# Moving the next token block's normalization and transposes later, and splitting the running sum of h*C into two tiles, in an adaLN + Mamba + mixture-of-experts kernel

## The chip, the cores and the metric

The kernel runs on one core of one Trainium2 chip. The metric is the device time of one execution in microseconds. TensorE (PE), VectorE (DVE), ScalarE (ACT), GpSimd (POOL) and SyncE (SP, which only issues DMAs) each run their own instruction stream in order and wait for one another through semaphores.

## The reference, cut to what matters

x has 4 sequences of 2048 tokens with 512 channels, in float32. Each sequence has six modulation vectors. The computation is

```
h  = layernorm(x) * (1 + ca) + sa
x1 = x + ga * mamba(h)
out = x1 + gb * moe(layernorm(x1) * (1 + cb) + sb)
```

In `mamba`, `z = h @ W_in` is split into val and gate, val goes through a convolution over 3 tokens and a SiLU and becomes u, and `B`, `C`, `Delta` are projections of u. For each of 512 channels and 16 states n:

```
abar_t = exp(Delta*A);   bbar_t = expm1(Delta*A)/(Delta*A + 1e-6) * Delta * B_t
h_t = abar_t * h_{t-1} + bbar_t * u_t
y_t = sum over n of h_t * C_t
out = (y * silu(gate)) @ W_out + residual
```

`moe` has one shared and eight routed experts (hidden size 256, exact GELU), two routed experts per token, every expert computed for all tokens and weighted by its gate.

## The kernel before, in words

Tokens are worked on in 16 blocks of 512 (index q, or H in the code). Channels lie on the 128 partitions, in 4 groups. The scan works on tiles of 128 x 1024: one unit is 1024 (channel group, token) columns, it has 16 states, and there are 32 units. So there are 512 tiles, numbered c. The program is a list of slots, one for each c, and each engine's stream holds for each slot its part of the scan and its part of everything else. A window is 32 slots (two units, one block's worth of other work). I call slot r of window H the one with c = 32H + r. The other work in window H is for several blocks at once (`steps_of`): projections of block qa = H+2, preparation of block qn = H+3, and output projection and experts of blocks qf = H-2 and qp = H-3. In windows 2 to 13 one slot of the scan carries one step of the other work; before window 2 and after window 13 the ratio differs (`PACE`). In the first windows POOL also scales weights ("fold", L1418). The first two and the last two token blocks form scan blocks of their own with two half tiles per instruction.

What one tile c goes through:

- ACT (`act_batch`), four tiles at a time. A batch first makes four squares (L754), then two logarithms over two tiles each (L761), then for each tile `exps` (L763): an exponential (L767), a tanh into `th` (L772, three buffers) and `abar` (L776). Each switch between kinds of function costs a table load. Batch w of a window (w = 0 to 7) runs about the time of slots 4w to 4w+3 and makes the tiles that are four slots further on. Named places within a batch ("start", "half squared", "squared", "half logs", "logs", 0, 1, 2, 3) are where `act_steps` puts the other work. Before its tanh of tile c, ACT waits for `thinv_done`: POOL has used the buffer's tile before.
- POOL (`pool_slot`) in slot c: multiplies the finished state of tile c-1 by its C row (`times_C`, L1352/L1355; in those scan blocks that hand their state on, a small copy L1348 stands before it), then Newton and `pool_steps` work such as `gating` (L1441: hidden activations times gate rows, in slots 18, 19, 22, 23, 24, 29, 30, 31), then `weight(c+2)` (L1379: `inv` times `th`). In slots 1 and 17 `gate_y` follows (L1372: the sum times silu(gate)). Last comes `add_to_y(c-1)`: a DMA that POOL issues and that adds the tile h*C to the tile `ysum` (L1366; the first state of a unit is copied, L1363). Each add waits for the one before it to have landed.
- PE (`pe_slot`) in slot c broadcasts row c+1 of B into PSUM (L1150) when the scan of c-1 is done; then `pe_jobs` gives the matmuls of that slot. They share four PSUM banks. `bank_of` and `before` are worked out when the program is built, from `bank_held_to`, an estimate of when each job's result has been taken; a job waits until the result before it in its bank has been taken.
- DVE (`dve_slot`) in slot c: times weight (L1179), times ratio (L1186), B row of c+1 times u (L1167), the scan of c (L1197), plus abar for c+1 (L1173), then other steps.
- SP issues each load at its place in the list, behind waits. In slot 24 it loads a C row once the tile before is multiplied (L680), then a gate row (`load_gate_row`, L564, waits for the fifth `gating`, that of slot 24), and then `load_w1(qf, 8)` (L544), the last expert's first matrix, which the two PE jobs ("w1", 16) and ("w1", 17) of slot 26 need.

The part that moves is the preparation of block qn: ACT normalizes its x in `xa` (L964, at batch 5 "start"), PE transposes it in slots 21 and 22 (jobs "t", L1051), and ACT takes the four transposes to `hT` (L825, `take_t`, batch 5 "logs" and place 1). The job ("w1", qf, 12) of slot 23 gets the PSUM bank of transpose 2, ("w1", qf, 13) that of transpose 3. The transposed block is needed by the "val" jobs of slot 31.

Of the kernel before, what the change touches and what calls it, by code (L numbers as in the profile page):

```python
# [8 lines left out]
ALU = mybir.AluOpType  # L9
# [15 lines left out]
def adaln_mamba_moe(nc, x, W_val, W_gate, taps, W_BC, W_deltaT, delta_base, W_tau, A_log, W_out, gate_W, W1, b1, W2, b2,  # L25
# [52 lines left out]
    with ExitStack() as ctx:  # L78
# [41 lines left out]
        th = sb("th", [P, 3, TB])  # L120
        abar = sb("abar", [P, 4, TB])
        hs = sb("hs", [P, 4, TB])
        ysum = sb("ysum", [P, TB])
# [263 lines left out]
        y_summed, y_gated, carry_done = sem("y_summed"), sem("y_gated"), sem("carry_done")  # L387
# [355 lines left out]
        def act_batch(act, batch):  # L743
# [19 lines left out]
            def exps(c):  # L763
                u = unit(c)
                act.wait_ge(ln_done, c + 1)
                for cols, g in parts(u):
                    ins = s.activation(inv[:, c % 6, cols], inv[:, c % 6, cols], ACT.Exp, scale=-1.0,  # L767
                                       bias=ln_coef[:, c % N, g:g + 1])
                ins.then_inc(inv_done, 1)
                ge(act, thinv_done, c - 2)  # L770
                for cols, g in parts(u):
                    ins = s.activation(th[:, c % 3, cols], delta[:, u % 2, cols], ACT.Tanh, scale=halfA[:, c % N, g:g + 1])  # L772
# [43 lines left out]
        def act_steps(act, H, w, place):  # L816
            s = nc.scalar
            qa, qn, qf, qp = H + 2, H + 3, H - 2, H - 3

# [122 lines left out]
            if w == 6:  # L942
                if place == "start":
                    take_w1(qf, 6)
                if place == "half squared":
                    take_w1(qf, 7)
                if place == 0:
                    take_w1(qf, 8)
            if w == 5:
                if place == "logs":  # L950
                    take_t(qn, (0, 1))
                    gelu(qf, 1)
                if place == 1:
                    take_t(qn, (2, 3))
                if place == "start" and has(qn):
                    act.wait_ge(a_rstd, qn + 1)
                    for tt in range(TPB):
                        ins = s.activation(rstdA[:, tt, 1:2], momA[:, tt, 0:1], ACT.Identity, scale=rstdA[:, tt, 0:1])
                    ins.then_inc(a_shift, 1)
                    act.wait_ge(a_shift, 2 * qn + 1)  # L960
                    s.activation(rstdA[:, :, 1], rstdA[:, :, 1], ACT.Identity, scale=-1.0).then_inc(a_shift, 1)
                    act.wait_ge(a_shift, 2 * qn + 2)
                    for tt in range(TPB):
                        ins = s.activation(xa[:, tt, :], xa[:, tt, :], ACT.Identity, bias=rstdA[:, tt, 1:2], scale=rstdA[:, tt, 0:1])  # L964
                    ins.then_inc(a_xn, 1)
            if w == 7:
                if place == "start":
                    gelu(qf, 2)

        def pe_jobs(H, r):
# [18 lines left out]
        def bank_held_to(j, at):  # L991
# [5 lines left out]
            held = {"t": (22.2, 22.3, 23.1, 23.2), "val": (1.5, 2.5, 3.5, 3.9), "gate": (8.3, 8.4, 9.5, 9.6), "p": (10.9, 11, 11.4, 11.5),  # L997
# [37 lines left out]
        def pe_steps(pe, H, r):  # L1035
# [6 lines left out]
            def job(j):  # L1042
# [5 lines left out]
                if kind == "t":  # L1048
                    pe.wait_ge(a_xn, q + 1)
# [106 lines left out]
        def dve_slot(dve, c):  # L1156
# [180 lines left out]
        def pool_slot(pool, c):  # L1337
# [20 lines left out]
            def add_to_y(c):  # L1358
                if 0 <= c < NC:
                    pool.wait_ge(hC_done, c + 1)  # L1360
                    if c % N == 0:
                        ge(pool, y_gated, unit(c))
                        gp_.dma_start(ysum[:], hs[:, c % 4, :]).then_inc(y_summed, 16)  # L1363
                    else:
                        pool.wait_ge(y_summed, 16 * c)
                        gp_.dma_start(ysum[:], hs[:, c % 4, :], accum_op=ALU.add).then_inc(y_summed, 16)  # L1366

            def gate_y(u):
                if 0 <= u < NU:
                    pool.wait_ge(y_summed, 16 * N * (u + 1))  # L1370
                    pool.wait_ge(gate_ld, 16 * (u + 1))
                    gp_.tensor_tensor(gy[:], ysum[:], gy[:], ALU.mult).then_inc(y_gated, 1)  # L1372

            def weight(c):
                if 0 <= c < NC:
# [3 lines left out]
                    gp_.tensor_tensor(inv[:, c % 6, :], inv[:, c % 6, :], th[:, c % 3, :], ALU.mult).then_inc(thinv_done, 1)  # L1379
# [14 lines left out]
            times_C(c - 1)  # L1394

# [9 lines left out]
            add_to_y(c - 1)  # L1405
# [148 lines left out]
```

## Time and profile before

| | us |
|---|---|
| median of 3 runs | 4772.27 (4767.54 to 4777.16) |
| the profiled execution, own time | 4775.98 |
| its span, first to last instruction | 4774.2 |
| mean granted TensorE clock | 0.885 |

Busy time of each engine over the span: DVE 4043.6 us (85%), ACT 3976.1 (83%), PE 3867.6 (81%), POOL 3651.3 (76%). A window in the middle takes 262 to 269 us. The table and the busy shares are averages over stages with different limits: setup (to 220 us), windows 0 and 1 with the weight scaling (to 770 us), windows 2 to 12 (to 3680 us), window 13 (to 3937 us), the faster-paced end (to 4560 us) and the last expert work (to 4774 us). In the rows further down, a bracket after an instruction is the time that its engine sat idle before it, and what ended that.

### The profile page before, as it was taken

Reading aid. Unit: us, or ns where it says so; the run is one execution under the profiler, and the core shown is the slowest. Engines: PE = TensorE matmul, PEld = TensorE weight load, DVE = VectorE, ACT = ScalarE, POOL = GpSimd, SP = SyncE. Lnnn points to the kernel's source line nnn. Section 1 sums busy time; section 2 is a strip of 40 time slices with the busy share of each in tenths; the row PEclk is TensorE's granted clock in tenths of the full one; section 3 lists DMA queues with packets and bytes.
Section 4 is the critical chain, followed back from the end, with each engine's and each line's share of the span. In section 5 each row is a group of like instructions: output and inputs, shape, how many; then the busy total and the mean of one; then the engine's idle time right before and its main releaser. Section 6 shows DMA issues by size and latency. Waiting matters only on the chain.

```text
span 4774.2 us, 37136 instructions
## 1 busy us (share of the span) xinstructions
PE 3867.6 (81%) x9708; PEld 1620.4 (34%) x9708; DVE 4043.6 (85%) x3896; ACT 3976.1 (83%) x4394; POOL 3651.3 (76%) x2304
## 2 busy tenths in 40 slices
PE   6624514989898888899898988899898977989889
PEld 3201101334333333333343333333333333333344
DVE  1388799999998989999999989999998998788820
ACT  2688798999989898989989898999899897978811
POOL 0499988888888888788888888788888887767621
PEclk7856756999999999999999999899999998989889
DMA  3678868878787878788787878888887886667541
GB/s 131 218 232 260 247 151 223 223 230 254 223 254 217 257 224 258 213 246 249 224 258 218 250 220 259 238 254 228 238 255 218 240 227 160 181 169 193 154 132 66
DMA packets 352221, 1037.19 MB, mean 217 GB/s; under 512 B 41253, under 2 KB 44389, under 8 KB 344710
## 3 DMA queue, kind: packets, MB, share of 16 engines
q1 hardware_dynamic: 278282, 766.35, 47.0%
q0 software_dynamic: 73728, 268.47, 28.4%
q8 instruction: 78, 1.28, 0.1%
q14 instruction: 133, 1.09, 0.1%
HBM read 639.74 MB, written 126.51 MB: 160 GB/s over the span
## 4 chain that ended last, share of the span: by engine, by line
PE 27%; ACT 21%; issue 14%; DVE 12%; POOL 10%; DMA 8%; SPq 0%; POOLq 0%; DVEq 0%; ACTq 0%
PE ps L1113 11%; PE ps L1132 8%; DMA ysum<-hs 6%; ACT inv L761 4%; PE ps L1083 4%; POOL inv L1379 3%; DVE ps L1179 3%; DVE ps L1167 2%; ACT th L772 2%; DVE ps L1173 2%; ACT inv L754 2%; ACT abar L776 2%; ACT inv L767 2%; POOL hs L1352 2%; DVE hs L1197 1%
## 5 line engine op out<-in xcount | busy, mean ns | idle before, releaser
L1379 POOL TENSOR_TENSOR inv<-inv,th 128x1024 f32<-128x1024 f32 x512 | 1261.4, 2464 | 203.7 <-ACT th L772 202.6
L1113 PE MATMUL ps<-hf,w1r 128*128 128x512 f32 x2304 | 1133.5, 646 | 135.0 <-ACT hT L825 69.9
L1352 POOL TENSOR_TENSOR hs<-hs,Cb 128x1024 f32<-128x1024 f32 x384 | 972.2, 2532 | 34.0 <-DVE hs L1197 17.5
L1150 PE MATMUL ps<-Brow,pick 48*128 48x512 bf16 x1024 | 342.5, 418 | 621.9 <-DVE hs L1197 620.9
L1132 PE MATMUL ps<-w2r,hid 128*128 128x512 f32 x1776 | 815.1, 606 | 0.9 <-DVE x L1236 0.9
L1167 DVE SCALAR_TENSOR_TENSOR ps<-ps,us 128x1024 f32<-128x1024 f32 x512 | 628.4, 1227 | 215.7 <-PE ps L1150 215.4
L754 ACT ACTIVATE inv<-nrd,kappa 128x1024 f32<-128x1024 f32 (+1 forms) x640 | 578.5, 967 | 188.2 <-DVE ps L1179 187.9
L1366 POOL DMA_DIRECT2D ysum<-hs x480 | 437.2, 911 | 355.4 <-DMA ysum<-hs 344.4
L1113 PEld LDWEIGHTS ps<-hf,w1r 128*128 128x128 f32 x2304 | 459.3, 206 | 730.3 <-issue 596.8
L1186 DVE SCALAR_TENSOR_TENSOR ps<-nrd,inv_kappa,ps 128x1024 f32<-128x1024 f32 (+1 forms) x640 | 675.2, 1073 | 15.6
L1197 DVE TENSOR_TENSOR_SCAN hs<-abar,carry,ps 128x512 f32<-128x512 f32 (+1 forms) x384 | 683.6, 1802 | 0.3
L776 ACT ACTIVATE abar<-delta,negA 128x1024 f32<-128x1024 f32 (+1 forms) x640 | 606.5, 967 | 83.2 <-DVE hs L1197 83.2
L1179 DVE SCALAR_TENSOR_TENSOR ps<-ps,inv 128x1024 f32<-128x1024 f32 x512 | 628.0, 1226 | 46.2 <-POOL inv L1379 23.1
L1173 DVE SCALAR_TENSOR_TENSOR ps<-abar,ps 128x1024 f32<-128x1024 f32 x512 | 618.8, 1209 | 21.2 <-ACT abar L776 21.1
L767 ACT ACTIVATE inv<-inv,ln_coef 128x1024 f32<-128x1024 f32 (+1 forms) x640 | 607.9, 969 | 1.5
L772 ACT ACTIVATE th<-delta,halfA 128x1024 f32<-128x1024 f32 (+1 forms) x640 | 605.9, 966 | 0.2 <-POOL inv L1379 0.2
L1197 DVE TENSOR_TENSOR_SCAN hs<-abar,ps 128x1024 f32<-128x1024 f32 (+1 forms) x256 | 511.7, 2009 | 0.3
L1132 PEld LDWEIGHTS ps<-w2r,hid 128*128 128x128 f32 x1776 | 333.1, 192 | 452.7 <-issue 447.5
L761 ACT ACTIVATE inv<-inv 128x2048 f32<-128x2048 f32 x256 | 479.2, 1903 | 1.4
L1150 PEld LDWEIGHTS ps<-Brow,pick 48*128 48x128 bf16 x1024 | 58.5, 96 | 982.0 <-DVE hs L1197 765.0
L1355 POOL TENSOR_TENSOR hs<-hs,Cb 128x1024 f32<-128x1024 f32 x128 | 310.8, 2428 | 36.2 <-DVE hs L1197 28.1
L1236 DVE TENSOR_TENSOR x<-ps,x 128x512 f32<-128x512 f32 x256 | 172.0, 683 | 171.6 <-PE ps L1132 150.8
(155 smaller groups left out, 5052.9 us busy)
## 6 DMA issues: line engine op xcount, KB each, us to landing
ysum<-hs POOLq DMA_DIRECT2D x512, 512.0 KB, 5.5
Cb<-c_rows SPq DMA_DIRECT2D x384, 512.0 KB, 4.5
w1r<-in_W SPq DMA_DIRECT2D x144, 512.0 KB, 5.7
w2r<-w_scaled SPq DMA_DIRECT2D x141, 512.0 KB, 7.3
Cb<-c_rows SPq DMA_DIRECT2D x128, 256.0 KB, 3.9
gbc<-expert_gates SPq DMA_DIRECT2D x128, 256.0 KB, 5.2
aw<-in_W_val SPq DMA_DIRECT2D x64, 256.0 KB, 6.5
xa<-in_x SPq DMA_DIRECT2D x32, 512.0 KB, 7.4
```

The lines of the kernel that those rows point to most:

```text
L767: ins = s.activation(inv[:, c % 6, cols], inv[:, c % 6, cols], ACT.Exp, scale=-1.0, bias=ln_coef[:, c % N, g:g + 1])
L772: ins = s.activation(th[:, c % 3, cols], delta[:, u % 2, cols], ACT.Tanh, scale=halfA[:, c % N, g:g + 1])
L776: ins = s.activation(abar[:, c % 4, cols], delta[:, u % 2, cols], ACT.Exp, scale=negA[:, c % N, g:g + 1])
L1113: mm = t.matmul(o, w1r[:, n % 2, k, h * P:(h + 1) * P], hf[:, k, :], start=(k == 0), stop=(k == G - 1))
L1132: mm = t.matmul(o, hidden(e)[:, h, tt * P:(tt + 1) * P], (last_w2(e) if q == NQ - 1 and grp == 1 else w2r[:, e % 3])[:, h, :], start=(grp ...
L1167: v.scalar_tensor_tensor(X(c), X(c), 1.0, us[:, u % 2, :], ALU.mult, ALU.mult).then_inc(uB_done, 1)
L1173: v.scalar_tensor_tensor(X(c), abar[:, c % 4, :], 1.0, X(c), ALU.add, ALU.mult).then_inc(p1_done, 1)
L1179: v.scalar_tensor_tensor(X(c), X(c), 1.0, inv[:, c % 6, :], ALU.mult, ALU.mult).then_inc(pw_done, 1)
L1186: ins = v.scalar_tensor_tensor(X(c)[:, cols], nrd[:, u % 2, cols], inv_kappa[:, c % N, g:g + 1], X(c)[:, cols], ALU.add, ALU.mult)
L1197: ins = v.tensor_tensor_scan(hs[:, c % 4, cols], abar[:, c % 4, cols], X(c)[:, cols], 0.0 if begins(u) else carry[:, g, c % N:c % N + 1], ...
L1352: gp_.tensor_tensor(hs[:, c % 4, :], hs[:, c % 4, :], Cb[:, c % 2, :], ALU.mult).then_inc(hC_done, 1)
L1379: gp_.tensor_tensor(inv[:, c % 6, :], inv[:, c % 6, :], th[:, c % 3, :], ALU.mult).then_inc(thinv_done, 1)
```

## The change

- ACT: the xa normalization is split. Its small statistics steps go from batch 5 "start" to batch 5 place 1; the four tile normalizations go two to batch 5 place 3 and two to batch 6 place 2; the four `take_t` go to batch 7, "squared" and "logs".
- PE: the transposes go from slots 21 and 22 to slots 28 and 29, with new estimates for their banks. As a result ("w1", 12) gets the bank of ("w2", 0) from slot 20, and transposes 2 and 3 in slot 29 get the banks of transposes 0 and 1 from slot 28.
- `th` has two buffers instead of three, so that ACT's tanh of tile c waits for POOL's weight of tile c-2 instead of c-3.
- `ysum` has two tiles, for even and odd states, each with a semaphore. An add waits for the add two states before. `gate_y` first adds the two tiles on POOL (one more 128 x 1024 operation for each unit) and then multiplies.
- POOL: `add_to_y(c-1)` moves from the end of the slot to directly behind `times_C(c-1)`, except in slots 1 and 17.

```diff
-        th = sb("th", [P, 3, TB])
+        th = sb("th", [P, 2, TB])
-        ysum = sb("ysum", [P, TB])
+        ysum = sb("ysum", [P, 2, TB])
...
-                ge(act, thinv_done, c - 2)
+                ge(act, thinv_done, c - 1)
...
+            def normalize_x(q, tts):
+                if has(q):
+                    act.wait_ge(a_shift, 2 * q + 2)
+                    for tt in tts:
+                        ins = s.activation(xa[:, tt, :], xa[:, tt, :], ACT.Identity, bias=rstdA[:, tt, 1:2], scale=rstdA[:, tt, 0:1])
+                    ins.then_inc(a_xn, 1)
...
+                if place == 2:
+                    normalize_x(qn, (2, 3))
             if w == 5:
                 if place == "logs":
-                    take_t(qn, (0, 1))
                     gelu(qf, 1)
-                if place == 1:
-                    take_t(qn, (2, 3))
-                if place == "start" and has(qn):
+                if place == 3:
+                    normalize_x(qn, (0, 1))
+                if place == 1 and has(qn):
...
             if w == 7:
+                if place == "squared":
+                    take_t(qn, (0, 1))
+                if place == "logs":
+                    take_t(qn, (2, 3))
...
-                20: [("w1", qf, 11), ("w2", qf, 0)], 21: [("w2", qf, 1), ("t", qn, 0), ("t", qn, 1)],
-                22: [("w2", qf, 2), ("t", qn, 2), ("t", qn, 3)], 23: [("w2", qf, 3), ("w1", qf, 12)],
+                20: [("w1", qf, 11), ("w2", qf, 0)], 21: [("w2", qf, 1)],
+                22: [("w2", qf, 2)], 23: [("w2", qf, 3), ("w1", qf, 12)],
-                27: [("w2", qf, 4)], 28: [("w2", qf, 5)], 29: [("w2", qf, 6)],
+                27: [("w2", qf, 4)], 28: [("w2", qf, 5), ("t", qn, 0), ("t", qn, 1)], 29: [("w2", qf, 6), ("t", qn, 2), ("t", qn, 3)],
...
-            held = {"t": (22.2, 22.3, 23.1, 23.2),
+            held = {"t": (29.2, 29.3, 30.1, 30.2),
...
-                        dve.wait_ge(y_summed, 16 * (c - 3))
+                        dve.wait_ge(y_summed[c % 2], 16 * (c // 2 - 1))
...
             def gate_y(u):
                 if 0 <= u < NU:
-                    pool.wait_ge(y_summed, 16 * N * (u + 1))
+                    for odd in range(2):
+                        pool.wait_ge(y_summed[odd], 16 * (N // 2) * (u + 1))
+                    gp_.tensor_tensor(ysum[:, 0, :], ysum[:, 0, :], ysum[:, 1, :], ALU.add).then_inc(y_joined, 1)
+                    pool.wait_ge(y_joined, u + 1)
                     pool.wait_ge(gate_ld, 16 * (u + 1))
...
             times_C(c - 1)
+            if r not in (1, 17):
+                add_to_y(c - 1)
...
             if r in (1, 17):
                 gate_y(c // N - 1)
-            add_to_y(c - 1)
+                add_to_y(c - 1)
```

## Rows read from the trace of the kernel before

**Rows 1.** Busy time of windows 2 to 12 (start:end us, length, PE, PEld, DVE, ACT, POOL; clock, DMA)

```profile
770.00:3680.00 2910.00, 2577.92 (x6506) 1069.99 (x6504) 2737.74 (x2463) 2636.46 (x2637) 2425.84 (x1509) 0.93 0.83 238
```

**Rows 2.** What DVE waited for, windows 2 to 12: us, times, longest

```profile
DVE ps L1167 <- PE ps L1150: 105.6, 41, 7.8
DVE ps L1173 <- ACT abar L776: 21.1, 11, 4.1
DVE ps L1179 <- POOL inv L1379: 15.6, 15, 2.0
```

**Rows 3.** Timeline of DVE, slot 23 of windows 2, 8 and 12

```profile
973.95 1.23 DVE L1167 SCALAR_TENSOR_TENSOR ps<-ps,us 128x1024 f32<-128x1024 f32 x1 [6.25 <-PE ps L1150]
...
2549.68 1.23 DVE L1173 SCALAR_TENSOR_TENSOR ps<-abar,ps 128x1024 f32<-128x1024 f32 x1 [2.04 <-ACT abar L776]
2560.68 1.23 DVE L1167 SCALAR_TENSOR_TENSOR ps<-ps,us 128x1024 f32<-128x1024 f32 x1 [6.71 <-PE ps L1150]
...
3617.71 1.23 DVE L1167 SCALAR_TENSOR_TENSOR ps<-ps,us 128x1024 f32<-128x1024 f32 x1 [7.80 <-PE ps L1150]
```

**Rows 4.** Timeline of PE and ACT around slot 23 of window 8

```profile
2526.37 2.93 ACT L964 ACTIVATE xa<-xa,rstdA 128x512 f32<-128x512 f32 x4
2539.42 1.43 ACT L825 ACTIVATE hT<-ps,modc 128x512 f32<-128x512 f32 x2
2553.62 1.43 ACT L825 ACTIVATE hT<-ps,modc 128x512 f32<-128x512 f32 x2
2554.43 5.67 PE L1113 MATMUL ps<-hf,w1r 128*128 128x512 f32 x8 [6.99 <-ACT hT L825]
```

**Rows 5.** Timeline of all engines, slots 20 to 27 of window 13

```profile
3841.84 2.28 DVE L1197 TENSOR_TENSOR_SCAN hs<-abar,ps 128x1024 f32<-128x1024 f32 x1
3849.12 1.23 DVE L1167 SCALAR_TENSOR_TENSOR ps<-ps,us 128x1024 f32<-128x1024 f32 x1 [1.23 <-PE ps L1150]
3892.96 1.23 DVE L1179 SCALAR_TENSOR_TENSOR ps<-ps,inv 128x1024 f32<-128x1024 f32 x1 [2.20 <-POOL inv L1379]
3898.89 1.23 DVE L1167 SCALAR_TENSOR_TENSOR ps<-ps,us 128x1024 f32<-128x1024 f32 x1 [3.37 <-PE ps L1150]
3842.68 1.15 ACT L772 ACTIVATE th<-delta,halfA 128x1024 f32<-128x1024 f32 x1
3864.33 2.37 POOL L1379 TENSOR_TENSOR inv<-inv,th 128x1024 f32<-128x1024 f32 x1 [1.40 <-ACT th L772]
3878.21 2.36 POOL L1441 TENSOR_TENSOR hid<-hid,gbc 128x1024 f32<-128x1024 f32 x1
3880.97 0.45 SPq L544 DMA_DIRECT2D w1r<-in_W  x1
3889.41 8.91 PE L1113 MATMUL ps<-hf,w1r 128*128 128x512 f32 x16 [6.22 <-DMA w1r<-in_W]
```

**Rows 6.** What POOL waited for, whole span: us, times, longest

```profile
POOL ysum L1366 <- DMA ysum<-hs: 344.4, 134, 7.2
POOL ysum L1363 <- POOL gy L1372: 20.0, 31, 1.0
```

**Rows 7.** Groups of POOL instructions (busy us, mean ns | idle before)

```profile
L1372 POOL TENSOR_TENSOR gy<-ysum,gy 128x1024 f32<-128x1024 f32 x32 | 77.3, 2416 | 11.2 <-DMA ysum<-hs 11.1
```

**Rows 8.** Timeline, window 8: POOL slots 15 and 19, ACT and DVE slot 20

```profile
2491.46 0.90 POOL L1366 DMA_DIRECT2D ysum<-hs  x1 [1.79 <-DMA ysum<-hs]
2520.41 2.35 POOL L1379 TENSOR_TENSOR inv<-inv,th 128x1024 f32<-128x1024 f32 x1
2522.03 1.14 ACT L772 ACTIVATE th<-delta,halfA 128x1024 f32<-128x1024 f32 x1
2523.27 2.28 DVE L1197 TENSOR_TENSOR_SCAN hs<-abar,ps 128x1024 f32<-128x1024 f32 x1
```

**Rows 9.** What POOL waited for, 220 to 514 us: us, times, longest

```profile
POOL ysum L1366 <- DMA ysum<-hs: 10.8, 8, 2.2
```

**Rows 10.** The chain of waits: start us, us, what (window 11)

```profile
3357.39 10.21 DMA w1r<-in_W
```

More of the change, by code:

```diff
@@ L386, in adaln_mamba_moe @@
             sem("B_ready"), sem("uB_done"), sem("abar_plus_1_done"), sem("weighted_done"), sem("bu_done"), sem("scan_done"))
-        y_summed, y_gated, carry_done = sem("y_summed"), sem("y_gated"), sem("carry_done")
+        y_summed = [sem("even_states_summed"), sem("odd_states_summed")]
+        y_joined, y_gated, carry_done = sem("y_joined"), sem("y_gated"), sem("carry_done")
         a_stat, a_log, a_rstd, a_shift, a_xn = (
@@ L769, in exps @@
                 ins.then_inc(inv_done, 1)
-                ge(act, thinv_done, c - 2)
+                ge(act, thinv_done, c - 1)
                 for cols, g in parts(u):
-                    ins = s.activation(th[:, c % 3, cols], delta[:, u % 2, cols], ACT.Tanh, scale=halfA[:, c % N, g:g + 1])
+                    ins = s.activation(th[:, c % 2, cols], delta[:, u % 2, cols], ACT.Tanh, scale=halfA[:, c % N, g:g + 1])
                 ins.then_inc(th_done, 1)
@@ L961, in act_steps @@
                     s.activation(rstdA[:, :, 1], rstdA[:, :, 1], ACT.Identity, scale=-1.0).then_inc(a_shift, 1)
[L962 to L965, printed above, removed]
             if w == 7:
@@ L996, in bank_held_to @@
                 return at + 1.95
-            held = {"t": (22.2, 22.3, 23.1, 23.2), "val": (1.5, 2.5, 3.5, 3.9), "gate": (8.3, 8.4, 9.5, 9.6), "p": (10.9, 11, 11.4, 11.5),
+            held = {"t": (29.2, 29.3, 30.1, 30.2), "val": (1.5, 2.5, 3.5, 3.9), "gate": (8.3, 8.4, 9.5, 9.6), "p": (10.9, 11, 11.4, 11.5),
                     "bc": (14.6,), "t2": (12, 12.1, 12.6, 12.7), "log": (14.95,), "gT": (15.9,),
@@ L1048, in job @@
                 if kind == "t":
-                    pe.wait_ge(a_xn, q + 1)
+                    pe.wait_ge(a_xn, 2 * (q + 1))
                     for tt in range(TPB):
@@ L1360, in add_to_y @@
                     pool.wait_ge(hC_done, c + 1)
-                    if c % N == 0:
+                    if c % N < 2:
                         ge(pool, y_gated, unit(c))
-                        gp_.dma_start(ysum[:], hs[:, c % 4, :]).then_inc(y_summed, 16)
+                        gp_.dma_start(ysum[:, c % 2, :], hs[:, c % 4, :]).then_inc(y_summed[c % 2], 16)
                     else:
-                        pool.wait_ge(y_summed, 16 * c)
-                        gp_.dma_start(ysum[:], hs[:, c % 4, :], accum_op=ALU.add).then_inc(y_summed, 16)
+                        pool.wait_ge(y_summed[c % 2], 16 * (c // 2))
+                        gp_.dma_start(ysum[:, c % 2, :], hs[:, c % 4, :], accum_op=ALU.add).then_inc(y_summed[c % 2], 16)
             def gate_y(u):
                 if 0 <= u < NU:
-                    pool.wait_ge(y_summed, 16 * N * (u + 1))
+                    for odd in range(2):
+                        pool.wait_ge(y_summed[odd], 16 * (N // 2) * (u + 1))
+                    gp_.tensor_tensor(ysum[:, 0, :], ysum[:, 0, :], ysum[:, 1, :], ALU.add).then_inc(y_joined, 1)
+                    pool.wait_ge(y_joined, u + 1)
                     pool.wait_ge(gate_ld, 16 * (u + 1))
-                    gp_.tensor_tensor(gy[:], ysum[:], gy[:], ALU.mult).then_inc(y_gated, 1)
+                    gp_.tensor_tensor(gy[:], ysum[:, 0, :], gy[:], ALU.mult).then_inc(y_gated, 1)
             def weight(c):
@@ L1378, in weight @@
                     pool.wait_ge(th_done, c + 1)
-                    gp_.tensor_tensor(inv[:, c % 6, :], inv[:, c % 6, :], th[:, c % 3, :], ALU.mult).then_inc(thinv_done, 1)
+                    gp_.tensor_tensor(inv[:, c % 6, :], inv[:, c % 6, :], th[:, c % 2, :], ALU.mult).then_inc(thinv_done, 1)
             def newton(u, place):
```

## The prediction

> **What bounds the kernel now.** I read the busy times of windows 2 to 12 first: they take 2910 us of the 4774, and DVE is busy 2738 of them [rows 1]. The four elementwise operations and the scan of a slot are fixed work on DVE, so only DVE's idle time there can be won. The view of what DVE waited for says how much: 105.6 us for PE's B row, 21.1 us for ACT's abar, 15.6 us for POOL's weight, 142.3 us in all [rows 2]. POOL's waits for the sum's DMA look larger, 344.4 us over the span [rows 6], but they are idle time of an engine that is seldom waited for, and count only where they come through in those 15.6 us.
>
> Then the timeline of DVE, to see where in a window the waits lie. In each of the eleven windows slot 23 holds one pair: a wait for abar and a wait for the B row; in window 8 they are 2.04 and 6.71 us, and the B row wait is 6.25 us in window 2 and 7.80 in window 12 [rows 3]. The abar waits sum to the 21.1 us; the eleven B row waits of slot 23 sum to 72.5 of the 105.6 us. Together 93.6 us, 8.5 a window. The other 33.1 us are small waits: 6.5 us in slot 26, 5.4 in slot 20, the rest in slots 5, 6, 13, 15 and 19.
>
> The cause is in the timelines of PE and ACT. PE idles 6.99 us until ACT has taken transposes 2 and 3, because job ("w1", 12) needs that bank, and the B row is queued behind that job. ACT is late since its batch 5 starts with 2.93 us of normalization and has 1.33 us of `take_t` before its first tanh (two instructions that share 1.43 us with overlap) [rows 4].
>
> **What the change does, part by part.**
>
> *Normalization and transposes.* From before the first tanh of batch 5 go 2.93 us, 1.3 us of `take_t`, and the small statistics steps. ("w1", 12) now depends on a bank that DVE has emptied by slot 21. Both halves of the slot 23 stall lose their cause: +93.6 us (plus is time gained, here and below). The same ACT work returns in batches 5 to 7. In slot 29 transposes 2 and 3 wait for takes 0 and 1, behind four squares and a gelu on ACT, with the B row of slot 30 queued behind them on PE. Counting from the tanh of tile 31, ACT needs some 11 us to those takes, and they then come within 1 us of when DVE wants the row, on either side: between 0 and 1 us a window, I take 0.3, so -3 us.
>
> *What is late next.* Window 13 is an experiment that the trace of before holds already: there is no block to prepare, so neither normalization nor transposes. Slot 23 is clean there, but the window still loses 1.23 us in slot 20 and 2.20 and 3.37 us in slots 26 and 27 [rows 5]. Its chain can be read off: the tanh of tile 23 starts at 3842.68; POOL's weight of tile 24 starts at 3864.33, 21.65 later; the `gating` of slot 24 ends at 3880.57, 16.24 later; SP, which waited for it, issues the w1 load, and PE starts on it at 3889.41, 8.84 later; its two jobs and the B row take until 3898.89, 9.48 more. In sum 56.2 us. DVE has, from the scan of slot 20 (3841.84) to the same point, 57.05 us less its three waits of 6.80, so 50.25 us of work [rows 5]. The chain is simply longer than DVE's work, and the stall is what is left over. In windows 2 to 12 the stall of slot 23 covered it.
>
> *POOL's new order.* An add that waits for POOL's own product just before it starts 0.6 us late: the 31 such cases in the trace, each a copy behind the gate product, cost 20.0 us, 0.65 each and 0.58 at the least [rows 6]. Now nearly every add stands so. The bound from below is nothing (if the wait overlapped, though none of the 31 did), from above 1.0; I take 0.6. In the chain the two adds of slots 23 and 24 now stand before the `gating`: 56.2 + 2 x 0.6 = 57.4, and 56.8 in the six windows whose scan block does not hand its state on, since the copy falls away.
>
> *Two buffers of tanh, and the join.* Tanh 23 now waits for weight 21, POOL slot 19. In window 8 that weight ends at 2522.76, 0.5 us before the scan of slot 20, and tanh 23 starts 1.2 us before it, so today ACT would not wait for it much [rows 8]. But weight 21 moves: four exposed waits since the last point that ACT sets (slot 14), +2.4; the join in slot 17, one operation as long as the gate product, +2.4 [rows 7]; removed DMA waits, 1.79 in slot 15 of window 8 [rows 8], on average 2.4 a window, -2.4. So it ends about 1.8 us after that scan on average, and 3.7 to 5.6 in windows 4 and 5. The chain starts there.
>
> *The stall of a window, then,* is chain plus start less DVE's work: 57.1 + 1.8 - 50.8 (DVE's work is a little longer with block preparation) = 8.1 us, times 11 = 89 us. It replaces 93.6 + 6.5 + 5.4 = 105.5 us. After it POOL has caught up, and without its DMA waits it should not be late in slots 31 and 0: +15.6 us. Windows 2 to 12: 105.5 + 15.6 - 89 - 3 = +29 us.
>
> *The rest.* Window 13 has the same chain without anything won: its stall grows from 6.8 to 12.5, less the relief at its start; I take -6 us. In window 0 POOL with its weight scaling sets the pace: 27 exposed waits x 0.6 = 16 and one join 2.4, against 10.8 us of DMA waits removed [rows 9]; -8 us. The end, paced by PE, has slack at almost every weight; bounds +2 and -8, I take -3. The setup and the last expert work don't change. Other windows' slots 1 to 14: POOL's DMA waits go there too, but DVE did not wait for POOL; 0, and cover enough if they came back. ACT's tanh 3, 7 and 11 must wait up to 7 us for their buffer; ACT's waits for DVE in the following squares hide that. If that cover were gone it would be 2 to 5 us a window.
>
> Sum: 29 - 6 - 8 - 3 = +12 us. A third to a half of that is lost if some windows behave like window 5, where ACT is late in slot 18 too; I take +8. The profiled execution took 4775.98 us, 3.7 over the median; 4776 - 8 = 4768 there, and 4764 against the median of 4772.3.
>
> A rule bears on the removed waits. The trace shows that a sum's DMA lands late enough to make POOL wait 134 times [rows 6]. The Trainium skill, "DMA: Bandwidth & Descriptors", section "Anatomy of one DMA — SWDGE (gpsimd) path", fits such a DMA as 2.0 us plus bytes over 436e3; an estimate by it is 3.2 us for 512 KB, and then hardly any wait would be there to remove. The trace does not agree, so it is not used.
>
> **The rivals.**
>
> *The stall simply goes (gain 50 to 90 us).* For it: the removed cause is clear, and if the exposed wait is near nothing and tanh 23 is not held, the chain is 56.2 - 1.2 - 50.8 = 4.2 us too long, 46 us in all: 105.5 + 15.6 - 46 = 75, about 4700. Against it: the 31 cases [rows 6] and the join.
>
> *The w1 chain gets longer than what it replaces (slower).* Place: slots 20 to 27, through tanh 23, weight 24, the fifth `gating`, SP's w1 load. It decides from 0.7 us a window above my 8.1. The w1 load took 8.4 us in window 13 but 10.21 in window 11 [rows 10]; if two sums in flight slow it by 1.8 us, that is 12 x 1.8 = 22 us, and if tanh 23 starts another 1.7 us later, another 20: 4764 + 42 = about 4805. For it: the DMA engines are already busy 0.83 of the time [rows 1]. The Trainium skill, the same page, section "Issuing engines are not separate DMA queues", says that DMAs of all issuing engines run on the same 16 and interleave. By that the freed adds take their time from the w1 load; nothing in the trace of before can show it.
>
> *Nothing moves.* The chain's stall equals the old one within a microsecond a window: 4772.
>
> **How the numbers follow.** 0.2%, 9.5 us, is what can be told from no change. My forecast, that most of the stall moves to slots 26 and 27 and the time falls by 0 to 25 us: 0.45, half of it beyond 0.2%. The stall simply goes: 0.20. The chain gets longer: 0.28, nearly all beyond 0.2%. Some other way of no effect: 0.07. So faster 0.44, same 0.28, slower 0.28. Eight in ten: from 4700 (the first rival) to 4812 (the second).
>
> **What would show it.** Slot 23: no wait of DVE for B rows. Slots 26 and 27: new waits for PE behind a w1 load, and some for POOL; 7 to 9 us a window, more in windows 4, 5 and 13. POOL: the waits for the sum's DMA near zero, adds with 0.58 us before them, about 450 times. Weight 21 and tanh 23 back to back. Slot 30: waits for PE under 1 us. Window 0 longer by 5 to 10 us. The prediction is wrong if DVE still waits in slot 23, if slots 26 and 27 stay under 4 us, if another slot stalls by over 2 us in each window, or if the adds start without a gap.

## The result, and the profile after

The changed kernel took 4792.92 us (median of 7 runs, 4780.86 to 4796.62) against 4774.31 us before (7 runs, 4761.24 to 4778.66): ratio 1.0039, 95% interval 1.0024 to 1.0054. It is slower by 0.39%. I had forecast 4764 and faster. The profiled execution after took 4796.57 us, its span is 4794.7.

The views that answer to [rows 1] and [rows 2], of the changed kernel, windows 2 to 12: busy times, then what DVE, ACT and PE waited for (us, times, longest).

```profile
781.60:3694.00 2912.40, 2583.83 (x6500) 1073.31 (x6499) 2738.67 (x2463) 2632.85 (x2631) 2483.41 (x1531) 0.92 0.83 238
```

```profile
DVE ps L1176 <- PE ps L1159: 108.2, 53, 5.8
DVE ps L1188 <- POOL inv L1391: 18.4, 21, 1.4
DVE uu L1259 <- ACT uu L852: 11.9, 9, 2.0
DVE x L1245 <- PE ps L1095: 7.0, 3, 2.6
```

```profile
ACT th L773 <- POOL inv L1391: 99.0, 62, 5.8
```

```profile
PE ps L1122 <- DMA w1r<-in_W: 77.6, 11, 8.1
PE ps L1122 <- ACT hid L882: 38.8, 11, 4.8
```

DVE's busy time is what it was, 2738.67 us after 2737.74 [rows 1], and so is nearly its waiting time. The abar row of [rows 2] is gone, the B row's total is nearly what it was, and two new rows stand at the end. Where in a window the waits lie has changed. Summed over windows 2 to 12, counting DVE's waits of over 0.3 us each, every wait under the slot whose scan stands before it (the wait for the B row that `dve_slot` has in slot 27, say, lies between the scans of slots 26 and 27 and stands under 26):

| slot | before | after | forecast |
|---|---|---|---|
| 23 | 93.6 | 0 | 0 |
| 20, 25, 26 | 11.8 | 83.3 | 89 |
| 31, 0 (POOL's weight) | 15.6 | 0 | 0 |
| 0 (ACT's values) | 0 | 11.7 | 0 |
| 5, 6 | 10.4 | 28.5 | 10.4 |
| 15 | 1.3 | 14.2 | 1.3 |
| all | 142.8 | 144.7 | 114 |

The stretch is 2912.3 us long from scan to scan, 2909.3 before. Length less waits is 2767.6 and 2766.5; it lies between 2763 and 2770 in every kernel below but one (e11, 2777). So DVE's waits account for this stretch, and each experiment can be read by them. It grew by only 3 us. The rest of the loss is outside: window 0 grew by 9.6 us, window 13 by 6.6, the setup before the first scan by 2.7, the last window by 5.8, and the end shrank by 5.6.

The chain of the prediction, in window 8 after the change (start us, us, instruction, idle before):

```profile
2533.97 2.27 DVE L1206 TENSOR_TENSOR_SCAN hs<-abar,ps 128x1024 f32<-128x1024 f32 x1
...
2535.73 1.15 ACT L773 ACTIVATE th<-delta,halfA 128x1024 f32<-128x1024 f32 x1 [0.31 <-POOL inv L1391]
...
2557.18 2.36 POOL L1391 TENSOR_TENSOR inv<-inv,th 128x1024 f32<-128x1024 f32 x1 [3.08 <-ACT th L773]
...
2571.49 2.66 POOL L1455 TENSOR_TENSOR hid<-hid,gbc 128x1024 f32<-128x1024 f32 x1
...
2574.55 0.53 SPq L545 DMA_DIRECT2D w1r<-in_W  x1
...
2582.32 8.67 PE L1122 MATMUL ps<-hf,w1r 128*128 128x512 f32 x16 [6.59 <-DMA w1r<-in_W]
...
2584.90 1.23 DVE L1188 SCALAR_TENSOR_TENSOR ps<-ps,inv 128x1024 f32<-128x1024 f32 x1 [1.41 <-POOL inv L1391]
...
2591.56 1.23 DVE L1176 SCALAR_TENSOR_TENSOR ps<-ps,us 128x1024 f32<-128x1024 f32 x1 [4.10 <-PE ps L1159]
```

Tanh 23 starts 1.76 us after the scan of slot 20 (forecast 1.8); then 21.45 to weight 24 (21.65), 16.97 to the end of the `gating` (17.4), 8.17 to PE (8.84), 9.24 to DVE (9.48). Step by step it is the forecast chain, 57.6 us long where 58.9 was forecast (57.1 and a start 1.8 after the scan, both on average).

### The profile page after: what moved, and what is told of

Read it like the earlier page. It is cut to its first block, busy times and chain, and to the rows that moved or that the text cites. A ratio compares the mean times of both kernels' runs of the same rounds, so it can differ in the third digit from the quotient of the medians.

```text
span 4794.7 us, 37199 instructions
## 1 busy us (share of the span) xinstructions
PE 3871.0 (81%) x9708; PEld 1621.6 (34%) x9708; DVE 4049.3 (84%) x3896; ACT 3978.4 (83%) x4394; POOL 3733.0 (78%) x2336
## 4 chain that ended last, share of the span: by engine, by line
ACT 23%; PE 20%; POOL 19%; issue 12%; DVE 7%; DMA 5%; POOLq 0%; SPq 0%; DVEq 0%; ACTq 0%
PE ps L1122 9%; POOL inv L1391 6%; POOL hs L1361 6%; PE ps L1141 5%; ACT inv L762 4%; ACT inv L755 3%; PE ps L1092 3%; DMA ysum<-hs 2%; POOL hid L1455 2%; ACT th L773 2%; ACT inv L768 2%; DMA w1r<-in_W 2%; ACT abar L777 2%; ACT L768 2%; DVE ps L1176 1%
## 5 line engine op out<-in xcount | busy, mean ns | idle before, releaser
L1391 POOL TENSOR_TENSOR inv<-inv,th 128x1024 f32<-128x1024 f32 x512 | 1306.4, 2551 | 225.4 <-ACT th L773 225.0
L1361 POOL TENSOR_TENSOR hs<-hs,Cb 128x1024 f32<-128x1024 f32 x384 | 930.5, 2423 | 92.9 <-DVE hs L1206 77.3
L1141 PE MATMUL ps<-w2r,hid 128*128 128x512 f32 x1776 | 828.7, 615 | 4.1 <-ACT xn L882 2.3
L1195 DVE SCALAR_TENSOR_TENSOR ps<-nrd,inv_kappa,ps 128x1024 f32<-128x1024 f32 (+1 forms) x640 | 675.1, 1073 | 15.6
L1375 POOL DMA_DIRECT2D ysum<-hs x448 | 395.1, 882 | 146.9 <-POOL hs L1361 107.3
L1364 POOL TENSOR_TENSOR hs<-hs,Cb 128x1024 f32<-128x1024 f32 x128 | 305.9, 2390 | 41.1 <-DVE hs L1206 33.4
```

Of the source, the lines that this page charges most:

```text
L1141: mm = t.matmul(o, hidden(e)[:, h, tt * P:(tt + 1) * P], (last_w2(e) if q == NQ - 1 and grp == 1 else w2r[:, e % 3])[:, h, :], start=(grp ...
L1195: ins = v.scalar_tensor_tensor(X(c)[:, cols], nrd[:, u % 2, cols], inv_kappa[:, c % N, g:g + 1], X(c)[:, cols], ALU.add, ALU.mult)
L1361: gp_.tensor_tensor(hs[:, c % 4, :], hs[:, c % 4, :], Cb[:, c % 2, :], ALU.mult).then_inc(hC_done, 1)
```

## The experiments

Times are medians, with the ratio to the kernel before on the same chip and its 95% interval. The kernel before had medians of 4768 to 4774 beside them; where kernels are compared with each other to a few us, the difference of each from its own kernel before is the better measure. The first five take the change apart.

**e1: the move alone.** The kernel before with the diff's parts on `normalize_x`, `take_t`, the job table, `held` and `a_xn`; `th` keeps three buffers, `ysum` one, the adds their place.

> Only the normalization and the transposes move; three buffers of tanh, one tile for the sums and the old place of the adds stay. Theory H (holding): the move itself is worth about what the first forecast said, since the slot 23 stall goes (93.6 us) and a stall in slots 20 to 27 like that of window 13 (6.8 us a window, 75 us) comes in its place together with the old 6.5 + 5.4 us; so 30 us faster than before, ratio 0.9937, and slots 0, 5, 6 and 15 lose nothing new. Rival M (move): what is lost in slots 0, 5, 6, 15 comes from the moved work, which makes ACT late for the rest of the window; then this kernel is within 10 us of before or slower, ratio 0.998 to 1.004, with the small stalls of slots 5 and 15 in it.

4713.80 us, 0.9879 (0.9860 to 0.9897): 57 us faster than before, twice what theory H said. DVE's waits, windows 2 to 12:

```profile
DVE ps L1175 <- PE ps L1158: 65.3, 40, 5.0
DVE ps L1187 <- POOL inv L1387: 17.4, 14, 3.4
```

Slot 23 is clean, slot 26 takes 53.0 us, 4.8 a window, and slots 0, 5, 6 and 15 lose nothing new. The move is a good edit; M is refuted.

**e2: the other half.** Two tiles for the sums, their new place, the join, two buffers of tanh, without the move.

> Two tiles for the sums, the new place of the adds, the join and two buffers of tanh, but normalization and transposes stay in slots 20 to 22. Theory H: the small stalls in slots 0, 5, 6, 15 and 20 (about 45 us) and the longer window 0 (9.6) come from this half, less 15.6 us of weights in slots 31 and 0: 30 to 40 us slower than before, ratio 1.006 to 1.008. Rival M: this half costs only window 0 and gains the 15.6 us, so within 5 us of before, ratio 0.999 to 1.001.

4846.13 us, 1.0153 (1.0137 to 1.0169), 75 us slower, twice H's figure. The two halves sum to +18 us, what the change costs. The wait for abar in slot 23 grew from 21.1 to 37.0 us, and slots 0 (ACT's values), 5, 6 and 15 hold 66 us, where they held 12 before.

**e3: two buffers of tanh alone.**

```
-        th = sb("th", [P, 3, TB])
+        th = sb("th", [P, 2, TB])
...
-                ge(act, thinv_done, c - 2)
+                ge(act, thinv_done, c - 1)
```

> The kernel before with two buffers of tanh instead of three and nothing else. Theory H: ACT waits for POOL's weight at tanh 3, 7, 11 and 15 and passes that on to the work behind it in its queue: 15 to 30 us slower than before, ratio 1.003 to 1.006, and the trace has over 100 us of ACT's waits for the weight. Rival S (sums): the loss of the second half comes from the join, the place of the adds and the two transfers in flight, and two buffers of tanh alone cost under 5 us, ratio below 1.001.

4822.73 us, 1.0110 (1.0092 to 1.0128): 52 us, more than either theory had. Waits of DVE and of ACT in windows 2 to 12 of this kernel:

```profile
DVE ps L1173 <- ACT abar L776: 36.6, 11, 4.1
DVE uu L1250 <- ACT uu L844: 20.3, 10, 2.0
```

```profile
ACT th L772 <- POOL inv L1379: 118.5, 57, 6.7
```

**e4: the whole change, adds behind the weight as before.**

```
             times_C(c - 1)
-            if r not in (1, 17):
-                add_to_y(c - 1)
...
             if r in (1, 17):
                 gate_y(c // N - 1)
-                add_to_y(c - 1)
+            add_to_y(c - 1)
```

> The whole change, but each add stays behind the weight in POOL's order, as before. So no add waits right behind POOL's own product (0.33 us each, 440 of them), and the add lands about one weight (2.4 us) and up to a gating later. Theory H: the time of the changed kernel less what the exposed waits cost where POOL is late (slots 23 to 26, 15, 20 and window 0): 10 to 20 us faster than the changed kernel, 4773 to 4783, window 0 back by 8 us. Rival S: DVE's scan then waits for late landings, and the time is that of the changed kernel or above (4793 to 4810).

4769.47 us, 0.9997 (0.9987 to 1.0007): 23 us under the change, 20 with each against its own kernel before, and window 0 is back from 303.7 to 291.7 us. Theory H is right in direction on both and a few us short in size; S is refuted. But the chain over the w1 load did not get cheaper with the exposed waits gone from it: DVE's waits in slot 26 are 84.2 us here and 69.8 in the changed kernel.

**e7: the move with two buffers of tanh,** the rung between e1 and e4.

> The move and two buffers of tanh, one tile for the sums and the old place of the adds. Theory H (the hold adds up wherever the other half stands): two buffers cost 51.8 us on the kernel before, so 4714 + 45 to 52 = 4759 to 4766, and two tiles with late adds (4769.5) cost 4 to 10 us on top, for the join. Rival I (interaction): a third of the 52 us was the longer abar wait in slot 23 (15.5 us), which the move takes away, so 4740 to 4750, and the second tile with its join costs 20 to 30 us of its own.

4754.87 us, 0.9966 (0.9954 to 0.9977). Now the change is a ladder, each rung against its own kernel before: the move -57, two buffers +40, the second tile and its join +15, the early place of the adds +20, in sum the measured +19. H was 4 us too high and I 5 too low: two buffers cost about 11 us less on the move than on the kernel before. The longer abar wait of slot 23, which the move takes away, may be those 11 us; it isn't shown, since in e3 PE's busy time is also 30 us above that of the kernel before, at a mean granted clock of 0.92 in the stretch against 0.93.

The rung from e7 to e4 shows one more thing. The load of slot 24 for the last expert, whose landing PE waits for, in window 8 of e7 and then of e4:

```profile
2550.05 0.46 SPq L544 DMA_DIRECT2D w1r<-in_W  x1
...
2558.25 8.78 PE L1121 MATMUL ps<-hf,w1r 128*128 128x512 f32 x16 [7.74 <-DMA w1r<-in_W]
```

```profile
2549.26 0.47 SPq L545 DMA_DIRECT2D w1r<-in_W  x1
...
2558.68 10.12 PE L1122 MATMUL ps<-hf,w1r 128*128 128x512 f32 x16 [7.11 <-DMA w1r<-in_W]
```

From issue to landing it takes 8.07 and 9.29 us there, and 8.67 and 10.43 on average over windows 2 to 12; in e1 it takes 8.52 and in the changed kernel, with two tiles and early adds, 7.97. With two tiles and late adds this load is 1.8 us slower, and DVE's waits in slot 26 grow from 67.4 to 84.2 us.

**e8: hold only the last tanh of each batch.** Three buffers again, on e1:

```
-                ge(act, thinv_done, c - 2)
+                ge(act, thinv_done, c - 1 if c % 4 == 3 else c - 2)
```

> The move with three buffers of tanh, but the last tanh of each batch (tiles 3, 7, 11 to 31) waits as if there were two. Theory L: ACT works in batches of four, and the last tanh of a batch stands up to three slots ahead of the weight that it waits for; all of the cost of two buffers is there, and this kernel takes within 8 us of the move with two buffers (4755 to 4770). Rival E: the cost comes from all tanhs alike, or from the order in which the two buffers are used; then it is within a third of that cost over the move alone, 4714 to 4730.

4758.37 us, 0.9966 (0.9955 to 0.9978), the time of e7. The wait is the cause, not the memory saved, and the last tanh of a batch carries all of it that can be measured; E is refuted.

**e9: those tanhs later.** On e7; `exps` leaves out the tanh of tiles 3, 11, 19, 23 and 27, and the next batch issues it:

```
             at("start")
+            if 0 <= c0 - 1 < NC and (c0 - 1) % WIN in LATE_TANH:
+                tanh(c0 - 1)
             for c in states[0:2]:
```

> The move with two buffers of tanh (4754.9), but the last tanh of five of the eight batches of a window (tiles 3, 11, 19, 23, 27) is issued behind the first work of the next batch, so that it no longer stands ahead of the values of slot 0 and the abar of its own tile. Two buffers cost 41 us over the move alone; ACT's waits there are 25.0 us at tile 3 and 39.0 at tile 11 of windows 2 to 12. Theory L (what the held tanh delays is the work behind it in ACT's queue): 20 to 35 of the 41 us come back, 4720 to 4735. Rival B (the weight itself is late with two buffers, wherever the tanh stands): nothing comes back or it gets worse, 4750 to 4775.

4752.06 us, 0.9961 (0.9948 to 0.9974), the time of e7. The values' wait in slot 0 went (8.8 to 0), but slots 15 and 20 took 9.7 us more. ACT's waits for the weight fell from 90.6 to 39.9 us in windows 2 to 12 and nothing came back: the time lies in B's range, and theory L, as I had put it, missed. Whether the late weight of B is the reason, no view here shows; the length of the holds alone is not their price.

**e12 to e15: which hold costs.** On e1, the stricter wait for one pair of tiles each (`if c % WIN in (3, 7)` and so on).

> The move with three buffers of tanh; only tiles 3 and 7 of each window wait as if there were two. All eight last tanhs together cost 44.6 us (4758.4 against 4713.8). Theory L (each hold delays the work behind it in ACT's queue, and each costs where that work is late): the wait for the values of slot 0, 8.5 us in the trace with all eight, and little else, so 8 to 12 us: 4722 to 4726. Rival B (what counts is the late weight in the stretch where POOL also does the gatings): under 5 us, 4714 to 4718.

> Only tiles 11 and 15 wait. Theory L: ACT is late for the w1 jobs of slot 15 (PE's wait for it rose from 10.6 to 32.1 us, DVE's wait for the B row of slot 15 to 10.1), so 10 to 15 us: 4724 to 4729. Rival B: under 5 us.

> Only tiles 19 and 23 wait. Theory L: DVE's waits in slots 20, 25 and 26 rose by 2.5 + 2.3 + 12.7 us, so about 17 us: 4729 to 4733. Rival B: most of the whole, 30 to 40 us, 4745 to 4755, since weight 24 sits on the chain to the last w1 load.

> Only tiles 27 and 31 wait. Both theories: within 5 us of the move alone (4710 to 4719), as its trace shows DVE no later in slots 28 to 31 with all eight holds; if it costs more, tanh 31 holds the transposes' evacuation and the B row of slot 30 behind it.

| tiles held | us | ratio | interval | over e1 |
|---|---|---|---|---|
| 3, 7 | 4726.56 | 0.9917 | 0.9901 to 0.9934 | 12.8 |
| 11, 15 | 4742.89 | 0.9946 | 0.9932 to 0.9960 | 29.1 |
| 19, 23 | 4718.60 | 0.9891 | 0.9874 to 0.9908 | 4.8 |
| 27, 31 | 4725.10 | 0.9902 | 0.9886 to 0.9918 | 11.3 |

Half of it is tiles 11 and 15; 19 and 23, which feed the chain that I had feared, cost next to nothing, and the intervals of e14 and e15 overlap that of e1. L's size was nearly right for 3 and 7 alone, B's nowhere; for 27 and 31 both had less. Waits of ACT and of PE in windows 2 to 12, first of e1, then with tiles 11 and 15 held:

```profile
ACT inv L754 <- DVE ps L1187: 116.1, 23, 9.5
ACT hid L881 <- PE ps L1121: 58.9, 40, 2.7
ACT xa L839 <- PE ps L1065: 19.3, 11, 2.0
ACT abar L776 <- DVE hs L1205: 14.4, 10, 2.7
```

```profile
PE ps L1121 <- ACT hid L881: 21.0, 10, 2.9
```

```profile
ACT inv L754 <- DVE ps L1187: 90.2, 23, 9.4
ACT hid L881 <- PE ps L1121: 68.7, 42, 3.5
ACT th L772 <- POOL inv L1387: 57.6, 18, 6.8
ACT abar L776 <- DVE hs L1205: 7.0, 7, 1.8
ACT xa L839 <- PE ps L1065: 6.2, 4, 1.9
```

```profile
PE ps L1121 <- ACT hid L881: 32.1, 11, 4.8
```

This shows how far the cover reaches. ACT is held 57.6 us; its old waits, the squares' among them, shrink by 25.9 + 7.4 + 13.1 = 46.4, and its waits for PE grow by 9.8. The 21.0 that are left are as much as DVE loses: its waits rose from 81.9 to 102.9 us, 7.5 of the 21 in slot 15, 7 in slot 26, the rest in small pieces. In between stands PE, whose wait for `take_w1` in slot 15 rose from 10.6 to 28.9 us.

By tile the two holds differ. Tile 11 is held 44.8 us, and the waits that ACT had in slots 7 and 8 (for PE, abar and the squares) shrink by 44.7: all of it is covered. Tile 15 is held only 12.8 us, and no wait for the squares stands between it and the takes of slot 15, in e1 or here. The other kernels agree: where tiles 14 and 15 are held for 11 us or more in windows 2 to 12 (e2, e3, e6, e7, e8, e9, e13 and the changed kernel), DVE loses 7.5 to 16.8 us in slot 15, and in the others, where it is 2 us or less, 0 to 5.4. This may also be why e9 gained nothing, as its late tanhs leave tile 15 out. No run holds tile 15 alone, so that it carries the price of the pair is likely, and not shown.

**e5: the last w1 load earlier.** On e1:

```
             if r == 23:
                 load_w2(qf, 2 if qf == NQ - 1 else 1)
-            if r == 24:
                 load_w1(qf, 8)
```

> The move of normalization and transposes alone, and SP issues the last w1 load at the end of slot 23, behind the w2 loads, instead of in slot 24 behind the gating and the gate row. In the move alone PE is done with the two jobs that use this buffer about 6 us before SP issues the load, and the 16 jobs that follow wait 5 to 6 us for it, 59.7 us in windows 2 to 12; DVE's waits in slot 26 are 53 us there. Theory Q (SP's order holds the load, the chain of the prediction): the load goes out 5 to 6 us earlier, the 59.7 us go, and DVE's waits for the B row in slot 26 (37.8) with them; 30 to 45 us faster than the move alone, 4670 to 4685. Rival D (the DMA engines): behind three w2 loads the w1 load lands no earlier, or pushes the loads around it back; within 8 us of the move alone, 4706 to 4722. Rival G: gating and weight are the last link of slot 26, DVE then waits for POOL there, and only 10 to 15 us are gained.

4705.18 us, 0.9857 (0.9841 to 0.9874), the fastest of all, 9 us under e1. The load does land earlier, as Q had it, but G comes nearest: what is left in slot 26 is all for POOL, 16.3 us, as it was in e1 (15.3). Waits of DVE and of PE in windows 2 to 12:

```profile
DVE ps L1186 <- POOL inv L1386: 40.6, 31, 3.7
DVE ps L1174 <- PE ps L1157: 32.3, 34, 1.6
```

```profile
PE ps L1120 <- DMA w1r<-in_W: 22.9, 11, 4.8
```

The 37.8 us for the B row in slot 26 are gone, but only 10 of them show in the stretch: POOL is late in slots 31 and 0 instead, 21.7 us. PE's wait for the load fell from 59.7 to 22.9 us, so D's reason is refuted, though the time is within 1 us of D's range; DVE went on to the next late engine. (The interval overlaps that of e1.)

**e6 and e16: the same edit on the whole change, and on e4.**

> The whole change with the same earlier w1 load. PE's waits for that load are 77.6 us in windows 2 to 12 there, DVE's waits in slots 25 and 26 74.4. Theory Q: the part of them that is for the B row, 56.8 us, goes, and the kernel comes to 4735 to 4750, under the kernel before. Rival G: what then holds DVE in slot 26 is POOL, late by the two tanh buffers and the exposed waits, and less than 20 us are gained (4775 to 4790).

> The whole change with the adds behind the weight and the early w1 load, but no late tanhs: between the change with late adds (4769.5) and the mended one (4713.0). Theory C (the chain over the w1 load was the price): DVE's 81.0 us in slot 26 fall to about 21 as in the mended one, and most of the 56 us come from the load alone: 4718 to 4735. Rival T (the late tanhs): the load alone gives 5 to 15 us as it did with the early adds, since tanh 31 is held and the wait moves to the transposes of slot 29, and the kernel takes 4755 to 4765.

e6: 4787.22 us, 1.0031 (1.0019 to 1.0043), 3 to 6 us, which is within the noise. e16: 4714.72 us, 0.9882 (0.9865 to 0.9898), 52 to 55 us. (The profiled executions differ by 18 and 45: that of the changed kernel was among its slowest, that of e6 the fastest of its five.) The same load, moved the same way, is worth many times as much with the adds behind the weight. The trace of e6 in window 8 says why (slot 28 and the transposes of slot 29), then PE's row of windows 2 to 12:

```profile
2593.50 1.15 ACT L772 ACTIVATE th<-delta,halfA 128x1024 f32<-128x1024 f32 x1 [3.27 <-POOL inv L1390]
...
2604.01 1.43 ACT L832 ACTIVATE hT<-ps,modc 128x512 f32<-128x512 f32 x2
...
2604.83 1.97 PE L1059 MATMUL ps<-identity,xa 128*128 128x128 f32 x8 [6.71 <-ACT hT L832]
```

```profile
PE ps L1059 <- ACT hT L832: 67.5, 11, 6.7
```

POOL, late with its exposed waits, holds tanh 31 (28.5 us); ACT is late for `take_t`, PE waits for the bank, and DVE's wait of slot 26 stands in slot 29: its wait for the B row falls from 56.8 to 2.2 in slot 26 and grows from 1.1 to 44.7 in slot 29. With late adds tanh 31 is held 7.5 us, DVE's slot 26 falls from 84.2 to 25.4 us and slot 29 takes 14.3. The time of e6 lies in G's range, but neither Q nor G had the place; C is right for e16 (22.0 us for the B row in slot 26, 21 forecast), 3 us under its range.

**e10: late adds, early load, late tanhs.**

> The whole change with the adds back behind the weight, the last w1 load at the end of slot 23 and the five late tanhs. It asks whether two tiles for the sums are worth anything once what they cost is gone. Theory J (POOL's waits for the sum's DMA were hidden, so removing them gains nothing, and the join costs): above the move with the early w1 load alone (4705), 4715 to 4745. Rival P: POOL, free of these waits, is no longer late in slots 26, 31 and 0, and the kernel comes under it, 4680 to 4703.

4712.98 us, 0.9887 (0.9873 to 0.9900), as e16, 8 us over e5. That is between the ranges of J and P, 2 us under J's, and P is refuted: with everything mended this kernel is still no faster than e5. It also has two buffers of tanh where e5 has three, so the second tile's own share of the 8 us isn't separated; no run has two tiles for the sums with three buffers of tanh.

**e11: each add one slot later.**

```
             times_C(c - 1)
-            if r not in (1, 17):
-                add_to_y(c - 1)
+            if r not in (2, 18):
+                add_to_y(c - 2)
...
-            if r in (1, 17):
+            if r in (2, 18):
                 gate_y(c // N - 1)
-                add_to_y(c - 1)
+                add_to_y(c - 2)
```

> The whole change, but the add that stands behind each product with C is that of the tile before, whose product ended a slot earlier, so that it waits for nothing; joins and gate products move one slot on. Theory X (the exposed wait of 0.33 us for POOL's own product is what the early place costs): as fast as the change with late adds, 4765 to 4778, and window 0 back to about 292 us from 303.7. Rival Y (the cost of the early place is something else, such as the DMA's start in front of the weight): no faster than the change, 4785 to 4800.

4841.51 us, 1.0157 (1.0141 to 1.0172). It doesn't decide what it was made for. Window 0 fell from 303.7 to 296.3 us, 7.4 of X's 12 us, but the edit brought a wait of its own, the scan of slot 20 for the sum of tile 16, behind the moved join:

```profile
DVE hs L1206 <- DMA ysum<-hs: 46.4, 12, 5.6
```

## Why the prediction was wrong

*Slot 23, +93.6.* Right, all of it.

*What is late next, -89.* Right in place and mechanism, and in size: 83.3 us. Over windows 2 to 12 the tanh starts 1.40 us after the scan on average (1.8 forecast), then come 21.46 and 16.77 us; in windows 4 and 5, where I had it 3.7 to 5.6 us after the scan, it starts 1.75 and 1.77 after it. That e5, e6 and e16 take 37, 56 and 59 us from the wait of slot 26 by moving that load alone shows the chain. But e1, with nothing of the change except the move, already has 57.6 of the 83.3, where the first rival's sum for such a kernel gives 46.

*Window 13, -6.* 6.6 measured, for another reason. Its waits in slots 20, 25 and 26 grew from 6.8 to 8.1 us, not to 12.5; the rest came in slots 0, 5 and 15. That number was luck.

*Weights of slots 31 and 0, +15.6.* Came as forecast.

*Slot 30, -3.* PE did wait for the takes in slot 29 (23.6 us in 11 windows, where before it waited nothing), and DVE next to nothing.

*POOL's new order: 0.6 a case.* Mis-sized, and its reach underrated. What POOL waited for, whole span:

```profile
POOL ysum L1375 <- POOL hs L1361: 107.3, 329, 0.7
...
POOL ysum L1375 <- POOL hs L1364: 36.4, 111, 0.7
...
POOL ysum L1381 <- DMA ysum<-hs: 17.8, 14, 4.2
```

143.7 us over 440 adds, 0.33 each; the 0.58 at the least of [rows 6] held only behind the gate product. Window 0 was forecast 8 us longer and grew by 9.6, but with 28 cases at 9.2 us instead of 16 the forecast's own sum would have given 1: near by luck again, and e4 shows that the early place costs 12 us there. In all windows together it costs 20 to 23 us (e4). Part of what I had put at nothing is DMA: I had left the landing of a sum at 5.5 us. The median times from issue to landing, of the changed kernel and of e4 (KB each, us):

```profile
ysum<-hs POOLq DMA_DIRECT2D x512, 512.0 KB, 7.7
...
xn<-gated_y SPq DMA_DIRECT2D x16, 1024.0 KB, 8.9
```

```profile
ysum<-hs POOLq DMA_DIRECT2D x512, 512.0 KB, 6.3
...
xn<-gated_y SPq DMA_DIRECT2D x16, 1024.0 KB, 7.8
```

Before they were 5.5 and 7.7. The load of the gated y in slot 3 feeds the jobs of slot 4, and DVE's waits in slots 5 and 6 follow it. I had put the first slots of a window at "0, and cover enough"; in the changed kernel slots 5 and 6 lose 28.5 us, 18 more than before. The kernels with one tile for the sums lose 6.6 to 14.3 us there, with medians of 6.5 to 7.7 us for this load; those with two lose 10.9 (e4, 7.8), 22.8 (e16, 8.5), 26.9 (e6, 9.1), 28.5 (after, 8.9), 30.6 (e11, 8.3), 31.1 (e10, 9.5) and 36.7 (e2, 10.3). So it goes with the second tile, and not with the early adds alone, as e10 and e16 have late ones. The join isn't in the way: but for e11 the load is issued 21.0 to 21.3 us after the scan of slot 1 on average, with one tile or two, and lands 28.1 to 28.9 us after it with one tile and 29.5 to 31.8 with two. The transfers in flight, two sums at once among them, are the likely cause, but no run took them away alone: it is argued, not shown.

My second rival had the w1 load slowed by two sums in flight, by 1.8 us. In the changed kernel it is not slower (7.97 us on average, 8.52 in e1), so the rival was right about the sign and wrong about the place. In e4, where the adds are late, the same load is 1.8 us slower than in e7, as shown there: what the rival named shows in these runs with two tiles and late adds, and not with early ones. The Trainium skill, "DMA: Bandwidth & Descriptors", section "Issuing engines are not separate DMA queues", has the transfers of all issuers share the same engines; the traces agree for `ysum`, for the gated y and, with late adds, for w1 (8.67 to 10.43 us); with early adds w1 doesn't show it.

*Two buffers of tanh: nothing.* **This is the step that failed.** I wrote that ACT's tanh 3, 7 and 11 must wait up to 7 us for their buffer and that "ACT's waits for DVE in the following squares hide that. If that cover were gone it would be 2 to 5 us a window." The holds came as described (up to 5.8 us after, 6.7 in e3), the cover didn't suffice: +52 us on the kernel before, +40 on the move; in windows 2 to 12 DVE's waits grew by 47.9 (142.8 to 190.7) and 43.4 us (81.9 to 125.3), 4.4 and 3.9 a window. Some of that I had priced as the late start of the chain: of the 43.4 us, 18.4 stand in slots 20, 25 and 26 (57.6 in e1, 76.0 in e7). What I had at nothing is 8.8 us in slot 0, 13.1 in slot 15 and 6.1 in slot 29; in the changed kernel slot 0 (ACT's values) and slot 15 lose 11.7 and 12.9 us that were not there before. In the held pair 11 and 15, 36.6 of 57.6 us were covered. I had compared one hold with one wait, and had not asked for each hold which wait stands behind it. The squares wait at the head of a batch; work that stands ahead of them, as the values of slot 0, has no cover, and where the squares wait for nothing, as ahead of the w1 takes of slot 15, the hold goes through. This path is read from the traces of e7 and e13; e3, e7 and e8 show the price, and no run shows the path alone. I also looked for the price of the hold at tile 23, on the chain, and put a rival there; that pair costs 4.8.

With the bound that I wrote down, 2 to 5 us a window, the sum +12 becomes -10 to -43. The measured -18.6 lies in it, though not by these 22 to 55 us alone: slots 0 and 15 lose 24.6 us, and slots 5 and 6 the 18 whose cause is open. The range held the time; the chance of slower, 0.28, did not carry this bound, and was meant for another place.

*Open.* What the 15 us between e7 and e4 are: the profiled executions of the two have the same span (4760.3 and 4760.6), so no trace shows them. What the traces show is a trade: DVE waits 16.8 us more in slot 26, behind the slower w1 load, and 11.6 less in slot 15, where the hold of tiles 14 and 15 is gone; the join is added work on POOL. Why slots 5 and 6 are late with two tiles, beyond what is argued above. Why the four pairs sum to 58 us and all eight holds cost 44.6 is likely overlap, and wasn't tested.

## What to carry to other kernels

When a buffer is taken from an in-order engine, sum the holds over the loop against the waits that would absorb them, and look at what stands between the two in the queue; a hold can be hidden only from the work behind the absorbing wait. That is how the traces of e7 and e13 read; e8 is the test that puts a price on it. Take an edit of several parts apart before judging it: here one part was worth -57 us and the rest +75. And a stall that goes moves to the next queue in line; the same earlier load gave at most 6, 9 or some 55 us, by what was late next.

## What the runs showed that I had not expected

A DMA that POOL issues right behind its own product waits 0.33 us for it (440 cases, 143.7 us), 0.58 behind the gate product (31 cases, 17.9 us): small, but on an engine that is late. Two tiles for the sums lengthened the median landing of a 512 KB accumulating transfer from 5.5 to 6.3 us with late adds and to 7.7 with early ones, and only with the late ones the last w1 load by SP, 512 KB too, took longer in its old place, 10.43 us instead of 8.67 on average. And a stricter wait on three buffers (e8, 4758) costs what two buffers cost (e7, 4755), which makes it a way to price a buffer without touching memory.
